# Delta rule: another hand-written sequence of the same steps on TensorE, ScalarE, VectorE and GpSimd

## What is computed

```python
def step(S, inp):
    qt, kt, vt, at, bt = inp
    err = jnp.einsum('bhvk,bhk->bhv', S, kt) - vt
    S = at[..., None, None] * S - bt[..., None, None] * err[..., None] * kt[:, :, None, :]
    o = jnp.einsum('bhvk,bhk->bhv', S, qt)
    return (S, o)
...
q = _silu(_dwconv_causal(x @ Wq, conv_q_w, conv_q_b))     # k and v likewise
alpha = jax.nn.sigmoid(x @ Wa + ba)
beta = jax.nn.sigmoid(x @ Wb + bb)
o = _gated_delta(q, k, v, alpha, beta, scale)
o = (o - mu) * jax.lax.rsqrt(var + 1e-05) * ln_w + ln_b
o = (o * jax.nn.sigmoid(x @ Wg).reshape(B, T, H, DV)).reshape(B, T, H * DV)
return o @ Wo
```

## Time and profile before

| | us |
|---|---|
| median of 3 runs | 2073.97 |
| lowest, highest | 2073.57, 2085.83 |
| the profiled execution | 2075.61 |
| its span, first to last instruction | 2073.8 |

### The profile page before, as it was taken

One profiled execution on the slowest core, in us unless ns is written; L12 is line 12 of the kernel. 1 busy time (PEld: TensorE's weight loads), 2 busy tenths in 40 slices (PEclk: granted clock), 3 DMA queues, 4 the chain that ended last, 5 costly groups with the idle time before them and its releaser, 6 DMA issues. The chain is left out here.

```text
span 2073.8 us, 64658 instructions
## 1 busy us (share of the span) xinstructions
PE 1917.8 (92%) x27132; PEld 1440.7 (69%) x27132; DVE 1641.0 (79%) x3085; ACT 1300.4 (63%) x2822; POOL 739.1 (36%) x1005
## 2 busy tenths in 40 slices
PE   6589999998995799999999999999999999999777
PEld 4133333334784688888888888888888888888666
DVE  3699999982654678888888888988888888888456
ACT  1158888885432457667666666666766766766543
POOL 2333444444222223423433433432432432432223
PEclk9779999999996899999999999999999999999879
DMA  4301212111001011011011111111111111110011
GB/s 144 89 21 36 54 32 60 41 30 30 1 1 40 32 34 46 32 36 46 32 36 38 41 36 36 43 36 36 43 35 36 43 35 36 33 35 15 1 44 41
DMA packets 74175, 79.57 MB, mean 38 GB/s; under 512 B 13280, under 2 KB 60768, under 8 KB 73888
## 3 DMA queue, kind: packets, MB, share of 16 engines
q1 hardware_dynamic: 73888, 75.44, 12.4%
HBM read 66.11 MB, written 8.91 MB: 36 GB/s over the span
## 5 line engine op out<-in xcount | busy, mean ns | idle before, releaser
L1758 DVE SCALAR_TENSOR_TENSOR d_acc<-ps,d_par,d_acc 128x1023 f32<-128x1023 f32 (+2 forms) x288 | 363.6, 1262 | 15.7 <-ACT d_acc L1639 13.8
L1455 PE MATMUL ps<-x1p,d_wh 128*128 128x512 f32 x1024 | 357.9, 431 | 14.1 <-DVE d_acc L1758 9.6
L549 ACT ACTIVATE a_prob<-ps 128x512 f32<-128x512 f32 (+2 forms) x640 | 311.3, 560 | 90.7 <-PE ps L515 86.7
L571 DVE TENSOR_REDUCE a_mx<-ps 128x2 f32<-128x1024 f32 (+2 forms) x320 | 336.6, 1110 | 34.2 <-PE ps L499 21.6
L1639 ACT ACTIVATE d_acc<-ps,d_par 128x512 f32<-128x512 f32 x192 | 148.9, 776 | 141.4 <-PE ps L1455 137.2
L1389 POOL TENSOR_TENSOR d_og_l<-d_o_g,d_og_h 128x512 fp32r<-128x512 f32 x64 | 82.5, 1290 | 354.2 <-ACT d_og_h L1735 354.2
L1455 PE MATMUL ps<-x1p,d_wl 128*128 128x512 f32 x512 | 204.4, 399 | 0.0
L1455 PEld LDWEIGHTS ps<-x1p,d_wh 128*128 128x128 f32 x1024 | 172.7, 193 | 38.0 <-DVE d_acc L1758 10.5
L494 PE MATMUL ps<-k,q 48*128 48x512 bf16 (+3 forms) x768 | 142.5, 347 | 35.9 <-DMA k<-scratch_k 20.7
L515 PE MATMUL ps<-q,k 51*128 51x512 bf16 (+2 forms) x640 | 161.1, 365 | 6.1 <-ACT a_prob L549 3.7
L529 PE MATMUL ps<-a_prob,a_v 128*32 128x512 f32 (+3 forms) x1536 | 166.0, 505 | 0.2
(11 more groups left out here) (242 smaller groups left out, 4791.4 us busy)
## 6 DMA issues: line engine op xcount, KB each, us to landing
d_abc<-scratch_alpha SPq DMA_DIRECT2D x32, 512.0 KB
d_gb<-scratch_g SPq DMA_DIRECT2D x32, 512.0 KB, 3.9
d_wr<-in_dw SPq DMA_DIRECT2D x16, 512.0 KB, 4.9
scratch_q<-p_parts SPq DMA_DIRECT2D x24, 128.0 KB, 2.3
q<-scratch_q SPq DMA_DIRECT2D x32, 96.0 KB
scratch_y<-a_oT SPq DMA_DIRECT2D x64, 36.0 KB
x_tok<-in_x SPq DMA_DIRECT2D x2, 1024.0 KB
q<-scratch_q SPq DMA_DIRECT2D x32, 64.0 KB
```

What stands on the lines that cost most here:

```text
L549: inc(nc.scalar.activation(prob[:, y % PB, g:g + heads, off:], ps[:, PLACE["st", n, x], 0:heads * w].rearrange("p (h c) -> p h c", c=w), A ...
L571: inc(nc.vector.tensor_reduce(out, ps[:, bank:bank + 2, 0:heads * w].rearrange("p r (h c) -> p r h c", c=w), AX.X, ALU.max, negate=True), ...
L1455: last = nc.tensor.matmul(ps[:, bank, :], wp[g][:, k, i, :], x(part), start=(k == 0 and j == 0), stop=(k == KE - 1 and j == 2))
L1758: inc(nc.vector.scalar_tensor_tensor(acc[i][:, d:T], taps[:, 0:T - d], par[p][:, 4 * i + j:4 * i + j + 1], acc[i][:, d:T], ALU.mult, ALU.a ...
```

## The change

It replaces the four lists of `ORDER`. Each engine has the same steps as before (83 on TensorE, 45 on ScalarE, 58 on VectorE, 9 on GpSimd); no instruction, size, buffer or wait is another.

```diff
     "PE": """
-        O.gate.1.1 S.qd.1.0 O.ks.5 O.pw.4 S.qd.1.1 S.v_turn.0 O.w.5 X.o_turn.1 S.oc.1.0 S.oc.1.1 O.qs.5 O.pw.5 O.s.5 L.proj.1.0.0 L.proj.1.0.1
-        O.ks.6 S.y64 S.k_turn.0 O.w.6 L.proj.1.1.0 L.proj.1.1.1 O.qs.6 O.s.6 O.pw.6 S.z64 O.ks.7 S.v_turn.1 X.out.0 O.w.7 S.y128 O.qs.7 O.pw.7
-        S.k_turn.1 S.z128 L.proj.2.0.0 L.proj.2.0.1 L.proj.2.1.0 S.w.0 L.pair.0 S.s.0 L.pair.1 L.proj.2.1.1 S.ks.1 L.pair.2 L.pair.3 S.pw.0 S.w.1
-        S.gate.0.0 S.qs.1 S.s.1 S.gate.0.1 S.pw.1 S.ks.2 X.out.1 X.out.2 S.qs.2 S.w.2 L.sq.0.0 L.sq.0.1 S.s.2 S.pw.2 E.proj.0.0.0 E.proj.0.0.1
-        L.qd.0.0 E.proj.0.1.0 S.ks.3 L.qd.0.1 L.oc.0.0 S.w.3 X.out.3 E.proj.0.1.1 S.qs.3 S.s.3 S.pw.3 L.oc.0.1 L.sq.1.0 S.ks.4 S.gate.1.0 O.o_turn.0
-        S.w.4 S.qs.4 L.sq.1.1 S.s.4""",
+        L.proj.1.1.1 S.z64 O.s.6 S.v_turn.0 O.pw.6 S.k_turn.1 O.ks.7 S.y128 S.v_turn.1 O.qs.7 O.w.7 S.z128 O.pw.7 X.out.1 S.w.0 L.proj.2.0.0 S.s.0
+        S.pw.0 L.proj.2.0.1 S.ks.1 L.proj.2.1.0 L.pair.0 L.pair.1 L.proj.2.1.1 S.w.1 L.pair.2 L.pair.3 S.qs.1 S.s.1 S.gate.0.0 S.pw.1 S.gate.0.1
+        S.ks.2 S.gate.1.0 S.gate.1.1 S.w.2 X.out.2 S.qs.2 S.s.2 L.sq.0.0 L.sq.0.1 S.pw.2 E.proj.0.0.0 S.ks.3 L.qd.0.0 L.qd.0.1 S.w.3 S.qs.3
+        E.proj.0.0.1 S.s.3 E.proj.0.1.0 L.oc.0.0 L.oc.0.1 E.proj.0.1.1 S.pw.3 S.ks.4 O.o_turn.0 L.sq.1.0 L.sq.1.1 O.o_turn.1 S.w.4 L.qd.1.0 S.qs.4
+        S.s.4 L.qd.1.1 S.pw.4 S.ks.5 X.out.3 L.oc.1.0 S.w.5 S.qs.5 L.oc.1.1 S.s.5 S.pw.5 L.k_turn.0 E.proj.1.0.0 E.proj.1.0.1 L.y64 S.ks.6
+        E.proj.1.1.0 O.out.0 S.qs.6 S.w.6""",
     "ACT": """
-        O.z64 O.v_turn.1 X.pw.6 X.w.7 O.y128 S.silu.0 X.pw.7 O.z128 S.silu.1 S.tap.2.0 O.w.0 S.tap.2.1 O.pw.0 O.w.1 S.blocks O.gate.0 O.pw.1 O.w.2
-        S.sq.0.0 S.sq.0.1 X.norm.0 X.norm.1 O.pw.2 L.tap.0.0 O.w.3 L.tap.0.1 S.silu.2 O.pw.3 S.sq.1.0 O.w.4 S.sq.1.1 X.o_turn.0 O.gate.1 S.v_turn.0
-        O.pw.4 O.w.5 X.o_turn.1 X.og.0 O.pw.5 S.diag L.tap.1.0 O.w.6 S.y64 L.tap.1.1 X.og.1""",
+        O.v_turn.1 X.w.7 O.z128 X.pw.7 O.w.0 S.silu.0 S.silu.1 O.pw.0 S.tap.2.0 S.tap.2.1 O.w.1 S.blocks O.pw.1 O.gate.0 O.w.2 X.norm.0 S.sq.0.0
+        S.sq.0.1 O.pw.2 O.gate.1 S.silu.2 O.w.3 X.norm.1 L.tap.0.0 L.tap.0.1 S.sq.1.0 S.sq.1.1 O.pw.3 O.w.4 X.o_turn.0 O.pw.4 X.o_turn.1 O.w.5
+        X.og.0 O.pw.5 S.diag S.y64 L.tap.1.0 O.w.6 L.tap.1.1 S.z64 S.v_turn.0 X.og.1 O.pw.6 S.y128""",
     "DVE": """
-        X.o_turn.0 S.oc.1.0 S.oc.1.1 O.s.5 O.ks.6 X.o_turn.1 O.pw.2 S.k_turn.0 O.pw.3 O.pw.4 O.s.6 L.conv.1.0 O.ks.7 O.pw.5 L.conv.1.1 L.conv.1.2
-        S.k_turn.1 O.pw.6 X.out.0 O.pw.7 L.decay S.s.0 L.pair.0 L.pair.1 S.ks.1 O.stats L.pair.2 L.pair.3 L.conv.2.0 S.s.1 L.conv.2.1 S.ks.2 L.first
-        L.conv.2.2 L.sq.0.0 X.out.1 S.s.2 L.sq.0.1 S.pw.0 L.qd.0.0 S.pw.1 S.ks.3 X.out.2 L.qd.0.1 L.oc.0.0 X.out.3 S.s.3 E.conv.0.0 S.ks.4 L.oc.0.1
-        L.sq.1.0 E.conv.0.1 S.s.4 L.sq.1.1 E.conv.0.2 S.ks.5 L.qd.1.0 L.qd.1.1""",
+        S.ks.1 L.pair.0 L.pair.1 O.stats L.pair.2 L.pair.3 S.s.1 L.conv.2.0 S.ks.2 L.conv.2.1 L.first L.conv.2.2 S.s.2 L.sq.0.0 L.sq.0.1 S.pw.0
+        S.ks.3 L.qd.0.0 X.out.2 L.qd.0.1 S.s.3 S.pw.1 L.oc.0.0 L.oc.0.1 S.ks.4 E.conv.0.0 L.sq.1.0 L.sq.1.1 E.conv.0.1 S.s.4 L.qd.1.0 L.qd.1.1
+        S.ks.5 E.conv.0.2 O.o_turn.0 L.oc.1.0 L.oc.1.1 S.s.5 X.out.3 O.o_turn.1 S.ks.6 S.pw.2 S.pw.3 S.pw.4 L.k_turn.0 S.pw.5 O.out.0 S.s.6
+        E.conv.1.0 S.ks.7 E.conv.1.1 S.pw.6 L.k_turn.1 E.conv.1.2 S.pw.7 O.out.1 L.s.0 E.decay""",
     "POOL": """
-        X.wo X.stats S.blocks S.one L.split X.og.0 S.qg X.og.1 L.scalars""",
+        S.one L.split X.wo X.og.0 S.qg L.scalars X.og.1 O.stats L.blocks""",
```

## The result

| | before | after |
|---|---|---|
| median of 22 runs each, us | 2077.57 (2073.57 to 2091.57) | 2084.38 (2079.55 to 2098.61) |
| ratio after to before, 95% interval | | 1.0031 (1.0019 to 1.0043) |
| span of the profiled execution, us | 2073.8 | 2089.1 |
| stage length, decay to decay, 5th to 32nd unit, us | 39.46 | 39.71 |

The change costs 0.31%, some 6.4 us. The forecast was +5.5 us on the time before, with stages of 39.65 us. The 22 runs of the kernel before have their median 3.6 us above that of the three runs shown ahead of the prediction, so in absolute terms the forecast of 2079 stands 5.4 under the measured 2084.4, inside the range of 2062 to 2097.

What follows compares the result with a forecast made beforehand. The prediction took TensorE's streaming plus its waits to set the stage. (-0.29 + 0.48) x 29 stages = +5.5 us on the profiled span of 2073.8 gave 2079, with 8 in 10 from 2062 to 2097.

Steps and rivals of the forecast that it cites:

- What bounds the kernel: Delta rule: TensorE's own work sets the 39.46 us stage; waits that other engines end add 0.6 us a stage.
- fill and drain: The delta rule outside its 29 full stages: taken as no change, 4 us either way.
- og.1 behind scalars, +0.48: GpSimd's og.1 holds the port shared with VectorE; decay is 0.99 us late, TensorE's pair.2 waits 0.48 us a stage.
- The walk from pw.7: Times counted from TensorE's pw.7: decay starts 2.85, ends 6.15; pair.0's bank free 7.10; pair.2 reached at 6.62 us.
- sq.0.0, its wait gone: TensorE's largest wait, for VectorE's first, goes: 5.97 us of cover against a chain of 5.75, 0.2 to spare.
- TensorE's floor, -0.29: Half of TensorE's 0.6 us of waits a stage is won: 39.17 from 39.46, late weight loads being partly hidden.
- Tight within 0.1 us: Three places given no price: s.0 behind w.0, qd.1.0 behind VectorE's sq.1.0, proj.0.0.0 behind conv.2.2.
- The same floor because of 12 runs in both lists: TensorE has 12 runs of small-tile steps in both lists, each such neighbour costing 0.10 us, so the floor is unchanged.
- The second rival: GpSimd's qg takes the port ahead of VectorE's o_turn.1; w.6 0.44 us late a stage: 2092, or 2098; chance 0.20.
- The first rival: VectorE gets the port first and og.1 waits, no collision: 2066, or 2056 with all waits gone; chance 0.22.
- Stages of 39.6: Sign that the forecast is right: delta-rule stages of 39.6 us; a stage under 39.1 would show it wrong.
- Half of o_turn at 0.65: Sign on VectorE: half of the o_turn instructions take 0.65 us; half above 2.2 would show the forecast wrong.

Runs made afterwards that it cites:

- all_small: Kernel after with og.1 ahead of scalars on GpSimd, qs.4 ahead of qd.1.0 and oc.1.0, oc.1.1 side by side on TensorE: 2064.61 us, 0.9929 of before.
- experiment 1: Kernel after with og.1 moved ahead of scalars on GpSimd: 2073.38 us, ratio 0.9969 to the kernel before.
- experiment 3: Kernel after with qg (1024 elements) instead of og.1 (512) directly behind scalars on GpSimd, og.1 ahead: 2123.65 us, ratio 1.0203 to the kernel before.
- experiment 4: Kernel before with GpSimd's last two entries swapped, so og.1 stands behind scalars: 2082.72 us, ratio 1.0005 to the kernel before.
- experiment 6: Kernel after with TensorE's oc.1.0 and oc.1.1 in one run behind qs.5, 11 small-tile runs instead of 12: 2077.81 us, ratio 1.0003 to before.
- experiment 7: Kernel after with VectorE's pw.2 moved ahead of o_turn.1, which so comes later: 2092.31 us, ratio 1.0057 to the kernel before.

## Why the prediction was right, point by point

- **What bounds the kernel: right.** The stage is TensorE's streaming plus its waits, and the ten experiments stand in the order of their stages, within their intervals. In size, 29 times the stage overstates the larger gains: for all_small it gives 20 us, the delta rule's length from first to last TensorE instruction 16.5 (1318.1 to 1301.6), the ratio 15. Some 3 us go back in fill and drain, which I had bounded with 4 either way and did not follow.
- **og.1 behind scalars, +0.48: right in mechanism and in size.** Measured +0.49 in the trace and 0.47 by taking it away (experiment 1). The walk from pw.7 was right to 0.05 us in each of its points. Two small things it didn't have: w.1, which needs ks.1 behind decay, is late too, but pays only 0.01; and of the 0.49 only 0.38 stands ahead of pair.2, where the forecast had all of its 0.48, and 0.10 comes between pair.2 and pair.3. So that it is right to 0.01 is in part luck. The rule on which it rests, that the port is held for a whole instruction, is shown by the two lengths: 1.0 us late behind 512 elements, 2.1 behind 1024 (experiment 3). That both halves of the change are needed is shown by experiments 1 and 4: the new order without the collision doesn't wait, the collision in the old order costs nothing. That in the new order it is the nearer pair.2 is read from the distances.
- **sq.0.0, its wait gone: right.** No L1504 row for `first` is left; 0.21 a stage won.
- **TensorE's floor, -0.29: near, one term missing.** All waits of the earlier trace rows went, 0.58 us a stage by their rows, and the stage got back 0.35 of it (0.21 at sq.0.0, 0.14 at ks.7). So about half was the right share, and the distances bear out the reason given, that a late weight load is partly hidden. Another 0.08 was won at y128; this and the 0.14 go back, by the trace, to the faster o_turn.1, for which the prediction counted no gain. But a place which the prediction had called tight and priced at nothing, qd.1.0 behind VectorE's sq.1.0, took 0.19 back: -0.21 - 0.14 - 0.08 + 0.19 = -0.24, against -0.29. That the sum came so near is in part compensation. The failing step is "Tight within 0.1 us" without a price; three such places at a coin toss each would have been worth a term.
- **The same floor because of 12 runs in both lists: right** in the count, but a run is worth 0.23, not 0.32 (experiment 6).
- **The second rival: did not occur, and was near.** o_turn.1 was forecast 2.5 us behind o_turn.0 and came at 2.49 (1225.71 to 1228.20). One short step more on VectorE makes it come true in part of the stages (experiment 7). A chance of 0.20 was fair. Its numbers were less good: the prediction's own 5.55 + 0.4 - 5.4 gives 0.55 a stage, not the 0.44 it wrote, and 0.35 was measured where it happens; and the edge was put at 0.1 us behind og.0's end, but o_turn.1 already loses when it starts 0.03 ahead of that end (1258.32 against 1257.05 + 1.30).
- **The first rival: excluded** by decay at 3.31. It is what experiment 1 made: 2066 was its forecast, 8 us under before; the measured ratio gives 6.4 under, the stage 0.25 less where the rival had 0.29.
- **Stages of 39.6:** 39.71. **Half of o_turn at 0.65:** both, 0.68 and 0.77. **2079:** +0.27% was forecast on the time before, +0.31% measured.

What was not tried: the tight places s.0 behind w.0 and proj.0.0.0 behind conv.2.2 one by one; neither shows a wait for another engine in the kernel after. And the 0.14 at ks.7 and the 0.08 at y128 are read from the trace only; no run isolates them.
